# The outer exponential of a megakernel's attention in three blocks a group instead of seven units

## The chip, the cores and the metric

The kernel runs on one NeuronCore of one Trainium2 chip, as one launch. The metric is the device time in microseconds; the runs of the kernel before took 256.16, 258.83 and 258.78 us, median 258.78.

## What is computed

The input is x, 32 x 32 x 16 x 25 in float32. Three layers follow each other: a graph and temporal convolution block (L0), an attention layer and a recurrent layer with a batch norm in front of it. All weights are small, 32 x 32 for the most part. Only the attention matters for this change. Each of the 32 batches has 400 tokens (16 x 25) of 32 channels:

```
t = layernorm(t) over channels
Q = (t @ rot) @ WqT;  K = (t @ ent) @ WkT;  V = t @ WvT
dist2 = |Q|^2 + |K|^2 - 2 Q K^T
scores = exp(-dist2)                 # the inner exponential
attn   = softmax(scores, axis=keys)  # the outer exponential, then its sum
t = t + attn @ V
```

So two exponentials are taken of every one of 400 x 400 pairs of tokens in each batch. Behind it stands `t + ffn(layernorm(t))`, where the recurrence needs W x normalised with mean and variance over all tokens.

## The kernel before, in words

The 32 batches are worked in 8 groups (G) of 4 (NB). A group's channels fill the 128 partitions: 4 batches x 32 channels, 400 tokens on the free axis.

In the attention the scores lie with the keys on the partitions and the 400 queries on the free axis. A batch's 400 keys are 3 full tiles of 128 and 16 left over; the rest of all four batches shares one more tile. So a group has 13 tiles (TILES) of 128 x 400. They are handled in pairs, the units: units 0 to 5 have two tiles (800 elements a partition), unit 6 has one (400). Tiles 0 to 2 belong to batch 0, 3 to 5 to batch 1, 6 to 8 to batch 2, 9 to 11 to batch 3. The result of both exponentials, `prob`, is kept in SBUF for a whole group, twice (parity of the group).

The order is written out by hand on each engine, and semaphores count the steps:

- PE, `attend`: for each unit of group g `scores` (two bf16 matmuls per tile, in two PSUM slots that alternate; slot by slot PE waits for the inner exponential of two units before). Between these stand steps of older groups: `products(g-1, k)`, attention times V, behind units 1, 2, 4 and 5 (k = 0 to 3); `sums` and `tail_sums` of g-1 behind unit 3; `center2(g-2)` behind unit 4, `wx(g-3)` behind 5, `variance2(g-2)` behind 6. `products` with k reads the tiles k of all four batches, so k = 0 needs all up to unit 4, k = 1 and 2 up to unit 5, k = 3 unit 6. k = 0 also waits for `nrm_ready`, which is the quotient of the group before, because it overwrites the PSUM bank that the quotient reads.
- ACT, `weights`: `inner` of unit u (from PSUM to `prob`, `e1_done`), and behind it `outer` of unit u-1 (in place in `prob`, `p_ready`). The outer of unit 6 stands behind the next group's inner of unit 0. In between stand the three steps of the second layernorm, `norm2`: logarithm and exponential of group g-3 at units 0 and 1, square of g-2 at unit 4.
- DVE, `attend`: `add_tiles` of units 0 to 5 sums a batch's three full tiles (two adds a batch, `part_sum`); behind unit 0 `norm2(g-3)`; behind unit 2 `reciprocals(g-1)`, 2.65 us long, and `stats(g-3)` (bn_stats); behind unit 4 `quotient(g-1)` and `residual(g-1)`. `variance2(g-2)` on PE waits for `stats(g-3)`.

The first group's units are mixed with the last steps of the layers before (lines around L498). The instructions of the trace carry these lines: inner L457, outer L464, adds L671, reciprocal L680, quotient L687, bn_stats L701, scores L930, sums L941, tail sums L947, products L959 and L963, variance L976.

Of the kernel before, what the change touches and what calls it, by code (L numbers as in the profile page):

```python
# [32 lines left out]
G = B // NB  # L33
# [14 lines left out]
FULL = N // P  # L48
TAIL = N - FULL * P

TILES = NB * FULL + 1
UNITS = (TILES + 1) // 2
ADDS = NB * (FULL - 1)
PROB = TILES * N
RB = 8
# [24 lines left out]
def build(nc, x_tok, x, consts, out):  # L80
    with ExitStack() as ctx:
# [9 lines left out]
        def c_(name, rows=P):  # L91
            o, w = COLUMNS[name]
            return cst[0:rows, o:o + w]
# [53 lines left out]
        prob = [arena[:, o:o + PROB].rearrange("p (k n) -> p k n", k=TILES) for o in (0, at_1)]  # L147
# [72 lines left out]
        def tiles(u):  # L220

            return 2 * u, min(2 * u + 2, TILES)

        def slot(par, u):

            return (par * UNITS + u) % 2

# [15 lines left out]
        def _(sp):  # L243
# [22 lines left out]
            def load_operands(i, par):  # L266

                g = 2 * i + par
                sp.wait_ge(kq_stored[par], 96 * i + 96 + CREDIT_DMA)
                sp.wait_ge(e_stored, 16 * i + 16 + CREDIT_DMA)  # L270
                for dst, scratch, n in ((ka, dka, 4), (qa, dqa, 4), (kb, dkb, 2), (qb, dqb, 2)):
                    sp.dma_start(dst[par][0:n * C, :, :], scratch[bass.ds(g, 1)].rearrange(
                        "o (b c) (s n) -> (c s) (o b) n", b=NB, n=N)).then_inc(operands_in[par], 16)
                rows = de[bass.ds(i, 1)].rearrange("o (g h b r) n -> g h r (o b) n", g=2, h=2, b=NB)
                for h, (dst, row) in enumerate(((kb, 2 * C), (qb, 2 * C + 3))):
                    sp.dma_start(dst[par][row:row + 3, :, :], rows[par, h, 0:3]).then_inc(operands_in[par], 16)
# [17 lines left out]
            with sp.Fori(1, PAIRS) as i:  # L294
                for par in range(2):
                    sp.wait_ge(s_done, UNITS * (2 * i + par - 1))
                    load_operands(i, par)
# [65 lines left out]
        def _(act):  # L363
# [88 lines left out]
            def inner(g, par, u):  # L452

                act.wait_ge(s_done, UNITS * g + u + 1)
                lo, hi = tiles(u)
                o = 2 * slot(par, u)
                nc.scalar.activation(prob[par][:, lo:hi, :], ps[:, o:o + hi - lo, 0:N], ACT.Exp,  # L457
                                     scale=2.0).then_inc(e1_done, 1)

            def outer(g, par, u):  # L460
                act.wait_ge(e1_done, UNITS * g + u + 1)
                lo, hi = tiles(u)
                p = prob[par][:, lo:hi, :]
                nc.scalar.activation(p, p, ACT.Exp).then_inc(p_ready, 1)  # L464

            def norm2(g, step, banks=NORM_BANKS):

                if step == 0:
                    act.wait_ge(centered2, g + 1)
                    nc.scalar.activation(sq2, ps[:, banks[0], 0:N], ACT.Square).then_inc(sq2_ready, 1)  # L470
                elif step == 1:
                    act.wait_ge(var2_done, g + 1)
                    if banks[0] != NORM_BANKS[0]:
                        act.wait_ge(xl2_ready, g + CREDIT1)
                    nc.scalar.activation(rs2, ps[:, banks[1], 0:N], ACT.Ln, bias=c_("eps")).then_inc(ln2_ready, 1)
                else:
                    act.wait_ge(ln2_ready, g + 1)
                    nc.scalar.activation(rs2, rs2, ACT.Exp, scale=-0.5).then_inc(rs2_ready, 1)

            def weights(g, par):  # L480
                since = g if isinstance(g, int) else G
                if since > 1:
                    act.wait_ge(pv_done, g - 1)
                for u in range(UNITS):
                    if since == 1 and u == 2:
                        for h in range(2):
                            act.wait_ge(kq_stored[h], 96 * PAIRS + CREDIT_DMA)
                    inner(g, par, u)
                    if u:
                        outer(g, par, u - 1)  # L490
                    elif since > 0:
                        outer(g - 1, 1 - par, UNITS - 1)
                    if u in (0, 1) and since > 2:
                        norm2(g - 3, u + 1)
                    if u == 4 and since > 1:
                        norm2(g - 2, 0)


            for step, first, end in ((squares, 0, 2), (inverse_roots, 2, 3), (kq_firsts, 3, 5),
                                     (v_and_squares, 5, UNITS)):  # L500
                step(PAIRS - 1)
                for u in range(first, end):
                    inner(0, 0, u)
                    if u:
                        outer(0, 0, u - 1)
            for g in range(1, 4):
                weights(g, g % 2)
            with act.Fori(2, PAIRS) as i:
                for par in range(2):
                    weights(2 * i + par, par)  # L510
            outer(G - 1, 1, UNITS - 1)
            for step in range(1, 3):
                norm2(G - 3, step)
            for g in (G - 2, G - 1):
# [32 lines left out]
        def _(dve):  # L547
# [109 lines left out]

            def add_tiles(g, par, u):

                dve.wait_ge(p_ready, UNITS * g + u + 1)  # L660
                for t in range(*tiles(u)):
                    b, k = divmod(t, FULL)
                    if b == NB or k == 0:
                        continue
                    dst = psum[:, par, b, :]
                    if k == 1:
                        a = prob[par][:, t - 1, :]
                    else:
                        a = dst
                        dve.wait_ge(part_sum, ADDS * g + (FULL - 1) * b + k - 1)  # L670
                    nc.vector.tensor_tensor(dst, a, prob[par][:, t, :], ALU.add).then_inc(part_sum, 1)  # L671
# [31 lines left out]
            def attend(g, par):  # L703

                since = g if isinstance(g, int) else G
                if since > 1:
                    dve.wait_ge(psum_used, g - 1)
                for u in range(UNITS - 1):
                    add_tiles(g, par, u)
                    if since > 2 and u == 0:  # L710
                        norm2(g - 3)
                    if since > 0 and u == 2:
                        reciprocals(g - 1, first=since == 1)
                    if since > 2 and u == 2:
                        stats(g - 3)
                    if since > 0 and u == 4:
                        quotient(g - 1, first=since == 1)
                        residual(g - 1)
# [85 lines left out]
        def _(pe):  # L804
# [130 lines left out]
            def sums(g, par, first):  # L935

                pe.wait_ge(part_sum, ADDS * (g + 1))
                if not first:
# [4 lines left out]
                last.then_inc(psum_used, 1)  # L943

            def tail_sums(g, par):
                pe.wait_ge(p_ready, UNITS * (g + 1))
                mm_(ps[:, 5, 0:N], c_("tail_ones"), prob[par][:, TILES - 1, :], start=False, stop=True,  # L947
                    skip_group_check=True).then_inc(sums_done, 1)

            def products(g, par, k, first):  # L950

                if k == 0:
                    pe.wait_ge(vb_ready, g + 1)
                    if not first:
                        pe.wait_ge(nrm_ready, g)

                pe.wait_ge(p_ready, UNITS * g + (TILES - 1 - FULL + k) // 2 + 1)
                if k == FULL:
                    mm_(ps[:, 4, 0:N], vb[:, par, P * k:P * k + P], prob[par][:, TILES - 1, :], start=False, stop=True,  # L959
                        skip_group_check=True).then_inc(pv_done, 1)  # L960
                    return
                for b in range(NB):
                    mm_(ps[C * b:C * b + C, 4, 0:N], vb[:, par, P * k + C * b:P * k + C * b + C],  # L963
                        prob[par][:, FULL * b + k, :], start=(k == 0), stop=False, skip_group_check=True)
# [47 lines left out]
            with pe.Fori(2, PAIRS) as i:  # L1012
                for par in range(2):
                    g = 2 * i + par
                    pe.wait_ge(operands_in[par], 96 * i + 96)
                    attend(g, par)
            products(G - 1, 1, 0, False)
            center2(G - 2, LAST_BANKS[G - 2])
            wx(G - 3)
            sums(G - 1, 1, False)  # L1020
            tail_sums(G - 1, 1)
            variance2(G - 2, LAST_BANKS[G - 2])
            for k in range(1, FULL + 1):
                products(G - 1, 1, k, False)
# [139 lines left out]
```

## Time and profile before

| | |
|---|---|
| runs, us | 256.16, 258.83, 258.78 |
| median, us | 258.78 |
| span of the profiled execution, us | 256.3 |
| what lies around the span | not given apart; the lowest run is as long as the span |
| attention stage, groups 0 to 7 | about 90 to 193 us of the span |
| recurrence, from | 218.3 us |
| PE, ACT, DVE busy | 81%, 67%, 59% |
| mean granted clock of TensorE | 0.944 |

The page gives busy shares for the whole span, and forty slices of it. A stage of the kernel is read from the timeline of an engine, where each row has the start, the time until the result is written, and in brackets how long the engine stood idle before it and who ended that. Two rows of ACT or DVE overlap by some 0.1 us, so the price of an instruction in a row of them is the distance between starts, not its duration. Who waits for its result waits for the duration. The chain of waits follows the work that ended last backwards, and so names the instructions on which the end depends.

### The profile page before, as it was taken

Reading aid. Unit: us, or ns where it says so; the run is one execution under the profiler, and the core shown is the slowest. Engines: PE = TensorE matmul, PEld = TensorE weight load, DVE = VectorE, ACT = ScalarE, POOL = GpSimd, SP = SyncE. Lnnn points to the kernel's source line nnn. Section 1 sums busy time; section 2 is a strip of 40 time slices with the busy share of each in tenths; the row PEclk is TensorE's granted clock in tenths of the full one; section 3 lists DMA queues with packets and bytes.
Section 4 is the critical chain, followed back from the end, with each engine's and each line's share of the span. In section 5 each row is a group of like instructions: output and inputs, shape, how many; then the busy total and the mean of one; then the engine's idle time right before and its main releaser. Section 6 shows DMA issues by size and latency. Waiting matters only on the chain.

```text
span 256.3 us, 4008 instructions
## 1 busy us (share of the span) xinstructions
PE 208.7 (81%) x1186; PEld 106.6 (42%) x1186; DVE 151.3 (59%) x284; ACT 170.7 (67%) x307; POOL 27.5 (11%) x44
## 2 busy tenths in 40 slices
PE   0395998998998979598999899999995944998950
PEld 0272653643643535123334333334332211987850
DVE  0147639929929915959667777777776544001560
ACT  2127398599499598979899898989894222254540
POOL 6000000260140050521010100001000000000000
PEclk9997999999999999979999999999998895599996
DMA  6910010096994091786451606070000000000006
GB/s 246 299 45 27 14 54 0 8 314 197 295 306 136 30 330 42 255 267 173 97 163 35 192 2 182 18 194 1 0 0 0 0 0 0 3 0 0 0 8 251
DMA packets 26881, 26.81 MB, mean 105 GB/s; under 512 B 1550, under 2 KB 25806, under 8 KB 26740
## 3 DMA queue, kind: packets, MB, share of 16 engines
q1 hardware_dynamic: 26724, 25.51, 33.8%
q10 hardware_dynamic: 144, 1.13, 1.3%
q8 instruction: 7, 0.11, 0.2%
q14 instruction: 6, 0.05, 0.1%
HBM read 14.74 MB, written 11.88 MB: 104 GB/s over the span
## 4 chain that ended last, share of the span: by engine, by line
PE 39%; DVE 21%; ACT 19%; issue 9%; DMA 6%; SPq 3%; DVEq 0%; ACTq 0%
DVE arena L680 6%; ACT arena L457 5%; PE ps L1045 5%; PE ps L1050 5%; DVE arena L598 5%; ACT arena L464 5%; PE ps L930 4%; PE ps L856 3%; DMA cst<-consts 3%; PE ps L832 3%; SPq L261 2%; ACT arena L389 2%; PE ps L842 2%; PE ps L868 2%; PE ps L976 2%
## 5 line engine op out<-in xcount | busy, mean ns | idle before, releaser
L457 ACT ACTIVATE arena<-ps 128x800 f32<-128x800 f32 (+1 forms) x56 | 44.4, 795 | 8.1 <-PE ps L930 6.4
L464 ACT ACTIVATE arena<-arena 128x800 f32<-128x800 f32 (+1 forms) x56 | 46.3, 828 | 0.0
L930 PE MATMUL ps<-qa,ka 128*128 128x400 bf16 (+1 forms) x128 | 35.4, 340 | 3.2 <-ACT arena L457 2.9
L930 PE MATMUL ps<-qb,kb 96*128 96x400 bf16 (+1 forms) x128 | 35.3, 338 | 0.0
L671 DVE TENSOR_TENSOR psum<-arena 128x400 f32<-128x400 f32 x32 | 19.6, 611 | 14.7 <-ACT arena L464 14.7
L533 ACT ACTIVATE yb<-ps,small 128x160 f32 x40 | 13.8, 391 | 16.5 <-PE ps L1050 16.2
L671 DVE TENSOR_TENSOR psum<-psum,arena 128x400 f32<-128x400 f32 x32 | 19.5, 609 | 7.1 <-ACT arena L464 6.0
L963 PE MATMUL ps<-arena,vb 128*32 128x400 f32 x192 | 21.8, 530 | 1.2 <-issue 1.2
L680 DVE RECIPROCAL arena<-ps 128x400 f32<-128x400 f32 x8 | 21.2, 2651 | 1.3 <-PE ps L947 1.3
L930 PEld LDWEIGHTS ps<-qa,ka 128*128 128x128 bf16 (+1 forms) x128 | 10.4, 97 | 27.6 <-ACT arena L457 11.8
L856 PE MATMUL ps<-arena,cst 128*128 128x400 f32 x32 | 14.6, 584 | 6.5 <-DVE arena L598 6.5
L1045 PE MATMUL ps<-xl,wsc 128*128 x80 | 16.3, 331 | 2.2 <-DVE yb L766 1.2
L598 DVE COPY arena<-arena 32x400 f32<-32x400 f32 x48 | 17.2, 358 | 0.9
L1050 PE MATMUL ps<-yb,cst 128*128 x80 | 17.1, 340 | 0.0
L1045 PEld LDWEIGHTS ps<-xl,wsc 128*128 128x128 f32 x80 | 13.4, 211 | 3.2 <-issue 3.2
L616 DVE TENSOR_TENSOR arena<-ps,arena 128x400 f32<-128x400 f32 x8 | 4.2, 569 | 17.2 <-ACT arena L417 17.2
L930 PEld LDWEIGHTS ps<-qb,kb 96*128 96x128 bf16 (+1 forms) x128 | 10.4, 98 | 8.9 <-issue 4.9
L331 POOL TENSOR_TENSOR arena<-arena,cst 128x400 bf16<-128x400 f32 x4 | 4.6, 1146 | 86.6 <-ACT arena L436 86.6
L1050 PEld LDWEIGHTS ps<-yb,cst 128*128 128x128 f32 x80 | 13.2, 209 | 1.2
L402 ACT ACTIVATE t<-arena,small 128x400 f32 (+1 forms) x8 | 4.8, 629 | 12.7 <-DVE arena L608 12.7
L856 PEld LDWEIGHTS ps<-arena,cst 128*128 128x128 f32 x32 | 5.5, 202 | 15.2 <-DVE arena L598 14.5
L778 DVE TENSOR_TENSOR outs<-t,yb x10 | 7.4, 737 | 6.8 <-ACT yb L533 6.8
(138 smaller groups left out, 358.8 us busy)
## 6 DMA issues: line engine op xcount, KB each, us to landing
dka<-arena SPq DMA_DIRECT2D x16, 200.0 KB, 3.0
dqa<-arena SPq DMA_DIRECT2D x16, 200.0 KB, 3.1
ka<-dka SPq DMA_DIRECT2D x8, 400.0 KB
qa<-dqa SPq DMA_DIRECT2D x8, 400.0 KB
arena<-x_tok SPq DMA_DIRECT2D x4, 400.0 KB
t<-x SPq DMA_DIRECT2D x1, 1600.0 KB, 12.6
dkb<-arena SPq DMA_DIRECT2D x8, 200.0 KB, 3.3
dqb<-arena SPq DMA_DIRECT2D x8, 200.0 KB, 4.3
```

The lines of the kernel that those rows point to most:

```text
L457: nc.scalar.activation(prob[par][:, lo:hi, :], ps[:, o:o + hi - lo, 0:N], ACT.Exp, scale=2.0).then_inc(e1_done, 1)
L464: nc.scalar.activation(p, p, ACT.Exp).then_inc(p_ready, 1)
L533: nc.scalar.activation(yb[:, bass.ds(s + 1, 1), 4 * h:4 * h + 4, :].rearrange("p o g c -> p (o g c)"), ps[:, 4 * h + bank, 0:HALF], ACT.Si ...
L598: last = nc.vector.tensor_copy(*tap_input(par, j, k))
L671: nc.vector.tensor_tensor(dst, a, prob[par][:, t, :], ALU.add).then_inc(part_sum, 1)
L680: nc.vector.reciprocal(rden, ps[:, 5, 0:N]).then_inc(rden_ready, 1)
L832: last = mm_(ps[NB * CH * h:NB * CH * (h + 1), 2 * par, MT * tt:MT * tt + MT], xk[par][0:MT, o:o + NB * CH], mlo[:, h, :], start=True, sto ...
L856: mm_(ps[:, 2 * par + 1, 0:N], cst[:, o + P * j:o + P * j + P], tap_in[par][j], start=(j == 0), stop=False)
L930: last = mm_(ps[row:row + keys, bank, 0:N], kk[par][0:rows, b, o:o + keys], qq[par][0:rows, b, :], start=first, stop=not first, skip_group ...
L963: mm_(ps[C * b:C * b + C, 4, 0:N], vb[:, par, P * k + C * b:P * k + C * b + C], prob[par][:, FULL * b + k, :], start=(k == 0), stop=False, ...
L1045: mm_(ps[:, 4 * h + bank, 0:HALF], wsc[:, :], xl2[:, 4 * h:4 * h + 4, bass.ds(NC * s, NC)], start=True, stop=False)
L1050: mm_(ps[:, 4 * h + bank, 0:HALF], c_("vT"), yb[:, bass.ds(s, 1), 4 * h:4 * h + 4, :].rearrange("p o g c -> p (o g c)"), start=False, stop ...
```

## The change

The seven outer exponentials of a group are taken in three blocks: units 0 and 1 (tiles 0 to 3), 2 and 3 (4 to 7), 4 to 6 (8 to 12). Block 0 is issued behind the inner exponential of unit 2, block 1 behind that of unit 4, block 2 behind the next group's inner of unit 1. `p_ready` now counts three a group, and who waited for a unit waits for its block. Nothing else is moved.

```diff
--- before.py
+++ after.py
@@ -50,6 +50,7 @@
 
 TILES = NB * FULL + 1
 UNITS = (TILES + 1) // 2
+OUTERS = ((0, 2), (2, 4), (4, 7))
 ADDS = NB * (FULL - 1)
 PROB = TILES * N
 RB = 8
@@ -221,6 +222,10 @@
 
             return 2 * u, min(2 * u + 2, TILES)
 
+        def outer_of(u):
+
+            return next(n for n, (lo, hi) in enumerate(OUTERS) if lo <= u < hi)
+
         def slot(par, u):
 
             return (par * UNITS + u) % 2
@@ -457,10 +462,11 @@
                 nc.scalar.activation(prob[par][:, lo:hi, :], ps[:, o:o + hi - lo, 0:N], ACT.Exp,
                                      scale=2.0).then_inc(e1_done, 1)
 
-            def outer(g, par, u):
-                act.wait_ge(e1_done, UNITS * g + u + 1)
-                lo, hi = tiles(u)
-                p = prob[par][:, lo:hi, :]
+            def outer(g, par, n):
+
+                first, end = OUTERS[n]
+                act.wait_ge(e1_done, UNITS * g + end)
+                p = prob[par][:, tiles(first)[0]:tiles(end - 1)[1], :]
                 nc.scalar.activation(p, p, ACT.Exp).then_inc(p_ready, 1)
 
             def norm2(g, step, banks=NORM_BANKS):
@@ -486,10 +492,10 @@
                         for h in range(2):
                             act.wait_ge(kq_stored[h], 96 * PAIRS + CREDIT_DMA)
                     inner(g, par, u)
-                    if u:
-                        outer(g, par, u - 1)
-                    elif since > 0:
-                        outer(g - 1, 1 - par, UNITS - 1)
+                    if u == 1 and since > 0:
+                        outer(g - 1, 1 - par, 2)
+                    if u in (2, 4):
+                        outer(g, par, u // 2 - 1)
                     if u in (0, 1) and since > 2:
                         norm2(g - 3, u + 1)
                     if u == 4 and since > 1:
@@ -501,14 +507,14 @@
                 step(PAIRS - 1)
                 for u in range(first, end):
                     inner(0, 0, u)
-                    if u:
-                        outer(0, 0, u - 1)
+                    if u in (2, 4):
+                        outer(0, 0, u // 2 - 1)
             for g in range(1, 4):
                 weights(g, g % 2)
             with act.Fori(2, PAIRS) as i:
                 for par in range(2):
                     weights(2 * i + par, par)
-            outer(G - 1, 1, UNITS - 1)
+            outer(G - 1, 1, 2)
             for step in range(1, 3):
                 norm2(G - 3, step)
             for g in (G - 2, G - 1):
@@ -657,7 +663,7 @@
 
             def add_tiles(g, par, u):
 
-                dve.wait_ge(p_ready, UNITS * g + u + 1)
+                dve.wait_ge(p_ready, len(OUTERS) * g + outer_of(u) + 1)
                 for t in range(*tiles(u)):
                     b, k = divmod(t, FULL)
                     if b == NB or k == 0:
@@ -943,7 +949,7 @@
                 last.then_inc(psum_used, 1)
 
             def tail_sums(g, par):
-                pe.wait_ge(p_ready, UNITS * (g + 1))
+                pe.wait_ge(p_ready, len(OUTERS) * (g + 1))
                 mm_(ps[:, 5, 0:N], c_("tail_ones"), prob[par][:, TILES - 1, :], start=False, stop=True,
                     skip_group_check=True).then_inc(sums_done, 1)
 
@@ -954,7 +960,7 @@
                     if not first:
                         pe.wait_ge(nrm_ready, g)
 
-                pe.wait_ge(p_ready, UNITS * g + (TILES - 1 - FULL + k) // 2 + 1)
+                pe.wait_ge(p_ready, len(OUTERS) * g + outer_of((TILES - 1 - FULL + k) // 2) + 1)
                 if k == FULL:
                     mm_(ps[:, 4, 0:N], vb[:, par, P * k:P * k + P], prob[par][:, TILES - 1, :], start=False, stop=True,
                         skip_group_check=True).then_inc(pv_done, 1)
```

ACT at the border between two groups, before (line 457 is `inner`, 464 `outer`, 475 and 478 the second layernorm's logarithm and exponential):

```order
L457 ACTIVATE arena<-ps 128x400 [waits s_done]
L464 ACTIVATE arena<-arena 128x800 [waits e1_done]
L457 ACTIVATE arena<-ps 128x800 [waits s_done,pv_done]
L464 ACTIVATE arena<-arena 128x400 [waits e1_done]
L475 ACTIVATE prep<-ps,cst 128x400 [waits var2_done]
L457 ACTIVATE arena<-ps 128x800 [waits s_done]
L464 ACTIVATE arena<-arena 128x800 [waits e1_done]
L478 ACTIVATE prep<-prep 128x400 [waits ln2_ready]
L457 ACTIVATE arena<-ps 128x800 [waits s_done]
L464 ACTIVATE arena<-arena 128x800 [waits e1_done]
```

ACT at the same place now (462 is `inner`, 470 `outer`):

```order
L462 ACTIVATE arena<-ps 128x800 [waits s_done]
L462 ACTIVATE arena<-ps 128x400 [waits s_done]
L462 ACTIVATE arena<-ps 128x800 [waits s_done,pv_done]
L481 ACTIVATE prep<-ps,cst 128x400 [waits var2_done]
L462 ACTIVATE arena<-ps 128x800 [waits s_done]
L470 ACTIVATE arena<-arena 128x2000 [waits e1_done]
L484 ACTIVATE prep<-prep 128x400 [waits ln2_ready]
L462 ACTIVATE arena<-ps 128x800 [waits s_done]
L470 ACTIVATE arena<-arena 128x1600 [waits e1_done]
```

The outer of unit 5 that stood between the inner exponentials of unit 6 and 0, that of unit 6 behind unit 0 and that of unit 0 behind unit 1 are gone; the block of units 4 to 6, 2000 elements wide, stands behind the inner exponential of unit 1, and the new group's first outer comes a unit later.

PE behind the second unit of scores of a group, now (936 is `scores`, 969 `products`; the order of PE is the same as before):

```order
L936 MATMUL ps<-qa,ka 128x400 [waits e1_done]
L936 MATMUL ps<-qb,kb 128x400
L936 MATMUL ps<-qa,ka 128x400
L936 MATMUL ps<-qb,kb 128x400
L969 MATMUL ps<-arena,vb 32x400 [waits p_ready,nrm_ready,vb_ready]
L969 MATMUL ps<-arena,vb 32x400 x3
L936 MATMUL ps<-qa,ka 128x400 [waits e1_done]
L936 MATMUL ps<-qb,kb 128x400
L936 MATMUL ps<-qa,ka 128x400
```

Nothing moved here. What `p_ready` stands for did: before, it was unit 4 of the group before at this place, now it is the block of units 4 to 6.

## Rows read from the trace of the kernel before

**Rows 1.** The page: the span, and each engine's busy time.

```profile
span 256.3 us, 4008 instructions
...
PE 208.7 (81%) x1186; PEld 106.6 (42%) x1186; DVE 151.3 (59%) x284; ACT 170.7 (67%) x307; POOL 27.5 (11%) x44
```

**Rows 2.** The chain of waits in order of time: start us, us on the chain, what.

```profile
177.05 2.25 DVE arena L680
...
179.62 0.53 DVE stat L701
...
180.28 0.91 PE ps L976 x2
...
188.57 0.59 DVE psum L671
```

**Rows 3.** ACT's timeline: start us, us, engine, line, operation, out<-in, [idle before <-releaser].

```profile
112.07 0.84 ACT L457 ACTIVATE arena<-ps 128x800 f32<-128x800 f32 x1 [1.28 <-DMA dqb<-arena]
...
134.96 0.84 ACT L457 ACTIVATE arena<-ps 128x800 f32<-128x800 f32 x1
...
181.91 0.84 ACT L457 ACTIVATE arena<-ps 128x800 f32<-128x800 f32 x1 [0.91 <-PE ps L930]
182.65 0.53 ACT L464 ACTIVATE arena<-arena 128x400 f32<-128x400 f32 x1
183.07 0.59 ACT L475 ACTIVATE prep<-ps,cst 128x400 f32<-128x400 f32 x1
183.55 0.84 ACT L457 ACTIVATE arena<-ps 128x800 f32<-128x800 f32 x1
184.27 0.88 ACT L464 ACTIVATE arena<-arena 128x800 f32<-128x800 f32 x1
185.03 0.54 ACT L478 ACTIVATE prep<-prep 128x400 f32<-128x400 f32 x1
185.45 0.84 ACT L457 ACTIVATE arena<-ps 128x800 f32<-128x800 f32 x1
```

**Rows 4.** PE's timeline, around products and sums of one group.

```profile
181.03 0.33 PE L930 MATMUL ps<-qa,ka 128*128 128x400 bf16 x1
...
182.49 0.88 PE L963 MATMUL ps<-arena,vb 128*32 128x400 f32 x8
...
185.69 0.88 PE L941 MATMUL ps<-psum,cst 128*32 128x400 f32 x8
186.50 0.94 PE L947 MATMUL ps<-arena,cst 128*128 128x400 f32 x2
187.28 0.33 PE L930 MATMUL ps<-qa,ka 128*128 128x400 bf16 x1
```

**Rows 5.** DVE's timeline, reciprocal, add and quotient.

```profile
189.68 2.65 DVE L680 RECIPROCAL arena<-ps 128x400 f32<-128x400 f32 x1
...
193.26 0.57 DVE L671 TENSOR_TENSOR psum<-psum,arena 128x400 f32<-128x400 f32 x1
193.75 0.56 DVE L687 TENSOR_TENSOR sq<-ps,arena 128x400 f32<-128x400 f32 x1
```

**Rows 6.** Groups of ACT by form: line engine op, shapes xcount | busy us, mean ns | idle before.

```profile
L464 ACT ACTIVATE arena<-arena 128x800 f32<-128x800 f32 x48 | 42.1, 877 | 0.0
...
L464 ACT ACTIVATE arena<-arena 128x400 f32<-128x400 f32 x8 | 4.3, 532 | 0.0
```

**Rows 7.** PE's timeline behind three idle stretches.

```profile
94.57 0.94 PE L880 MATMUL ps<-arena,prep 128*128 128x400 f32 x2 [1.70 <-DVE arena L616]
...
106.39 0.33 PE L930 MATMUL ps<-qa,ka 128*128 128x400 bf16 x1 [2.69 <-ACT arena L457]
...
197.04 1.67 PE L970 MATMUL ps<-t,cst 128*128 128x400 f32 x2 [1.74 <-DVE xl L695]
```

**Rows 8.** Windows of PE: stretch, us, PE busy (count), PEclk, DMA share, GB/s.

```profile
108.30:111.70 3.40, 3.40 (x17) 0.51 0.97 331
...
197.10:200.50 3.40, 3.40 (x8) 0.51 0.00 0
```

## The prediction

> **What bounds the kernel now.** I read the page first. ACT is busy 67% of the span and PE 81% [rows 1], so neither share alone says what holds the attention stage, and the stage has to be read as a ring. The chain of waits in order of time gives it [rows 2]: reciprocal of a group, then bn_stats, then the variance matmul, then the first scores of the next group, then the exponentials, then two adds, then the next reciprocal. ACT's timeline gives the period: the inner exponential of unit 2 starts at 134.96 in group 3 and at 185.45 in group 7, four groups in 50.49 us, 12.62 each [rows 3]. The same rows add up to it: 177.05 to 185.45 from reciprocal to unit 2's inner exponential (8.40), 3.12 on to the adds at 188.57, 1.11 on to the next reciprocal at 189.68 [rows 2, 3, 5]. That is 12.63. In this ring the outer exponentials of units 6, 0 and 1 lie on ACT one after another, and only unit 2's has somebody waiting for it at once. PE is never held by an outer exponential: it meets products(g, 0) behind the scores of unit 1 of the next group, long after the unit 4 that it reads has been done.
>
> **The change, part by part.**
>
> *Fewer instructions.* Outers of 800 elements start 0.76 us before the next instruction on ACT (184.27 to 185.03), one of 400 elements 0.42 (182.65 to 183.07) [rows 3]. So 400 elements cost 0.34 and an instruction by itself 0.08. Four fewer in each of 8 groups are 32 x 0.08 = 2.6 us of ACT. A merged one lasts, by 532 and 877 ns [rows 6] and so 345 ns for each 400 more, about 1.57 us (1600) and 1.91 us (2000). These are extrapolations in one direction; at 300 or 390 ns instead of 345 the ring below changes by under 0.4 us. ACT still has idle time in every group, and others wait for what it writes. Here the page "Perfetto Trace Analysis" of the Trainium skill, section "Optimizing Scalar/DVE Operations", has two rules. Grouping helps if the engine is saturated (it puts 93 ns on a ScalarE instruction in SBUF, an estimate of 3.0 us for 32); if the engine isn't saturated and makes bubbles on others, breaking instructions up may finish work sooner. By the first the sum would be about minus 3, by the second a loss; my rows speak for the second.
>
> *The results come later.* This is the term that decides. The last block of a group (units 4 to 6) is computed behind the inner exponential of unit 1 of the next group. Before, units 4 and 5 were ready long before that. Three things want them:
> - PE's products(g, 0), in order behind scores(g+1, 1) and ahead of scores(g+1, 2), which ACT needs next. Behind PE's wait stand the scores, the sums and all else.
> - DVE's adds of unit 4, and behind them on DVE the quotient of group g-1. products(g, 0) waits for that quotient too.
> - The reciprocal, which stands behind the adds of unit 2; these now wait for the block of units 2 and 3, which runs behind inner exponential 4, not 3.
>
> So the old ring takes the new waits in. From one reciprocal to the next, at the full clock:
> 1. Reciprocal to inner exponential 1: 177.05 to 183.55 is 6.50 [rows 2, 3], less the outer of unit 6 that went from there, 0.42: 6.08. It holds variance and first scores, 180.28 to 181.91.
> 2. That inner 0.72 (183.55 to 184.27), the block of 2000 elements 1.91, and 0.04 until its reader starts (the 3.12 above less 0.72, 0.76, 0.72 and 0.88): 2.67.
> 3. Add 0.49 (193.26 to 193.75), quotient 0.57 [rows 5], and 0.13 to PE (bn_stats ends at 180.15, PE starts at 180.28 [rows 2]): 1.19.
> 4. PE from products 0 to the scores of unit 4: 182.49 to 187.28, 4.79, which holds two products, scores 2 and 3, sums and tail sums [rows 4]. Then the scores of unit 4, 0.88 (1.63 from variance to inner exponential less the 0.75 of the variance's own step, 180.28 to 181.03): 5.67. ACT can't be faster here, since inner exponentials 3 and 4 need those scores.
> 5. Inner exponential 4, 0.72, block of 1600 elements 1.57, and 0.04: 2.33.
> 6. Two adds, 188.57 to 189.68: 1.11.
>
> Sum 19.05, against 12.62: **6.4 us more a group**. Groups 3 to 7 are reached by four such rings: 25.7.
>
> *Before the ring is whole.* From unit 2 of group 1 to that of group 3 took 22.89 (112.07 to 134.96) [rows 3]. Group 1 to 2 anew: 3.98 to inner 4 (step 4 less 0.81 and 0.88), 0.72 and 1.42 for it and the block's place on ACT, 0.84 and 0.9 for inner 5 and the next scores, 0.74, then 2.67, 1.19, 0.81 and 0.88: 14.2. Group 2 to 3 adds a square, a logarithm and part of the variance, 15.6. Together 6.9 more. Reaching unit 2 of group 1: the block has to be waited for, about 3 us, but ACT has 1.28 idle for a DMA there, and arrives about a microsecond earlier: 1.8 more, at most 3, at least 0. At the end, from unit 2 of group 7 to its reciprocal, steps 4 to 6 give 7.4 in place of 4.2: 3.2 more; the path behind is as before.
>
> Sum at the full clock: 1.8 + 6.9 + 25.7 + 3.2 = **37.6**.
>
> *The clock.* PE now stands idle twice in a ring: about 2.5 us between the scores of unit 6 and the variance, which waits for bn_stats (scores 4 to 6 with what stands between them are some 5.0 us of PE's steps; by steps 4 to 6 and rows 2 the variance starts 0.88 + 2.33 + 1.11 + 3.23 = 7.55 after scores 4 do), and about 4.4 us ahead of products 0 (the last block 1.95, inner 1 and logarithm 1.2, add and quotient 1.2). In the trace before, an idle stretch of 2.69 us was followed, within two microseconds of its end, by 3.4 us at 0.51 of the clock, that is at 1.2 and not 2.4 GHz, one of 1.74 by the same again, one of 1.70 by nothing [rows 7, 8]. So I expect a low stretch in every ring. It costs half its length where PE is on the ring: 1.7 us in step 4. For variance and first scores (1.63) I count half of a second one, 0.8. That is 1.7 for each of the two early groups and 2.5 for each of four rings: **13.4**. From below the price is 0; from above it is all of PE's work on the ring at half clock, 4.79 + 0.88 + 1.63 = 7.3 a ring more, but no low stretch on busy PE here was so long; two whole ones of 3.4 plus the first scores give 4.9 a ring, 23 in all. The page "TensorE: Matmul & The Clock Gate" of the Trainium skill, Part 1, says that the low clock is the default and activity lifts it, which would make the low stretches come in every ring; the rows above agree, but show it only at single places.
>
> *What is hidden.* Nothing moves on SP and POOL. Operand loads wait for the scores of the group before, now later but with a longer group to land in. The blocks write the same tiles in place.
>
> Total 37.6 + 13.4 = 51.0. The profiled execution has a span of 256.3, about the lowest run (256.16); the median of the three runs is 2.5 above it. Against the span the new time is 307.3; with a part of that distance I say **308**.
>
> **The rivals.**
> A. *The forecast*, ring and low stretches: 299 to 318. **0.74**.
> B. *The ring at the full clock*: 256.3 + 37.6, so 293 to 299. For it: idle of 1.70 left the clock alone. Against it: 4.4 us is longer than any idle stretch that stayed free. **0.08**.
> C. *A shorter ring*: bn_stats is not the last thing the variance waits for, and the leg over the reciprocal drops out. Then a group takes inner 4 to inner 5 to the next scores, as in group 2 to 3, 15.6 to 16.4, and 4 x 2.7 to 4 x 3.4 go away: 280 to 284, with low stretches to 292. Against it: that leg already ends the wait before the variance, and its inputs come later now. **0.08**.
> D. *Worse*: both low stretches whole in every ring, or a wait that I have not seen: above 318. **0.07**.
> E. *Not slower*: ACT sets the pace, and the 32 saved starts come off: 256.3 - 2.6 = 253.7, at the least gain the same time. This is the grouping rule above. It decides at PE's products 0: it needs the last block to be done when PE gets there. But the block starts behind inner exponential 1, which reads the scores that PE has just finished, so it ends 0.72 + 1.91 us later at the least; PE would have to take matmuls out of order. **0.03**.
>
> "Faster", "same" and "slower" are meant at 1%, about what a measurement of this kernel can tell from no change. Faster and same share E: 0.02 and 0.01; slower 0.97. The range takes A and B and leaves C, D and E out: 293 to 318, 0.82.
>
> **What the new profile would show.** ACT's outer instructions: 24, mean 1.57 and 1.91 us. Step 1 to 6: 19 us at least from one unit 2 to the next in groups 3 to 7, near 21.5 with the low clock. PE's wait for the quotient (DVE) ahead of products 0, 4 us and more in each group, and one for bn_stats ahead of the variance of about 2.5. In the chain, products, sums and quotient would appear, which are not in it now. PEclk would show 0.5 to 0.9 all through the stage. I am wrong if groups come every 12 to 13 us, if PE's idle time ahead of products is under a microsecond, or if the clock stays at 1.0.

## The result, and the profile after

The change takes 1.206 times as long as the kernel before, 95% interval 1.197 to 1.216: median 313.85 us of four runs (308.83 to 314.36), against 258.07 before. Ratios here and below are taken over undisturbed runs alone (of the change only two, 313.41 and 308.83 us, which makes it 53 us slower), so they can differ from the quotient of two medians. The profiled execution has a span of 311.6 us, 55.3 more than the 256.3 before. The forecast was 308, with a range of 293 to 318.

The page first: span, busy times, and the slices of the granted clock.

```profile
span 311.6 us, 3962 instructions
...
PE 229.4 (74%) x1186; PEld 109.7 (35%) x1186; DVE 150.2 (48%) x284; ACT 169.4 (54%) x275; POOL 28.4 (9%) x44
...
PEclk9997999999999959596876875975967969559996
```

Before, ACT was busy 67% [rows 1]; now it is 54%, and its busy time is 1.3 us shorter (169.4 against 170.7). What was added on ACT is waiting. PE, with the same 1186 matmuls, is busy 229.4 us in place of 208.7, and PEclk now lies between 0.5 and 0.9 in most slices of the attention stage.

ACT by form: the merged instructions (line 470 is `outer` now). Last columns are the count, busy time, mean ns, and the idle time before them.

```profile
L462 ACT ACTIVATE arena<-ps 128x800 f32<-128x800 f32 x48 | 39.8, 838 | 59.6 <-PE ps L936 59.4
L470 ACT ACTIVATE arena<-arena 128x1600 f32<-128x1600 f32 x16 | 24.5, 1531 | 0.0
L470 ACT ACTIVATE arena<-arena 128x2000 f32<-128x2000 f32 x8 | 15.0, 1872 | 0.0
```

They took 1.53 and 1.87 us, where [rows 6] extrapolated to 1.57 and 1.91. Ahead of the inner exponentials of 800 elements ACT stands idle for 59.4 us in all, waiting for scores; before it was 5.1.

ACT's timeline, inner exponential of unit 2 in groups 1, 2, 3 and 7. It answers to the first two lines and the last of [rows 3].

```profile
113.76 0.84 ACT L462 ACTIVATE arena<-ps 128x800 f32<-128x800 f32 x1 [3.27 <-PE ps L936]
...
130.15 0.84 ACT L462 ACTIVATE arena<-ps 128x800 f32<-128x800 f32 x1 [4.23 <-PE ps L936]
...
148.45 0.84 ACT L462 ACTIVATE arena<-ps 128x800 f32<-128x800 f32 x1 [3.82 <-PE ps L936]
...
237.18 0.84 ACT L462 ACTIVATE arena<-ps 128x800 f32<-128x800 f32 x1 [4.04 <-PE ps L936]
```

Group 1 starts 1.69 us later than before. Groups 1 to 3 take 34.69 us in place of 22.89, the four groups from 3 to 7 take 88.73 in place of 50.49, so 22.18 each, and all behind unit 2 of group 7 takes 74.4 in place of 70.9. That is 1.7 + 11.8 + 38.2 + 3.6 = 55.3, the whole difference.

The chain of waits through one ring, from reciprocal to reciprocal. Columns: start us, us on the chain, what (L686 reciprocal, L707 bn_stats, L982 variance, L470 outer, L693 quotient, L969 products, L462 inner, L677 add).

```profile
200.77 0.37 DVE arena L686
...
203.34 0.53 DVE stat L707
...
204.00 1.43 PE ps L982 x2
...
208.74 1.89 ACT arena L470
...
211.23 0.58 DVE sq L693
...
211.93 1.56 PE ps L969 x8
...
220.30 0.84 ACT arena L462
...
222.59 0.59 DVE psum L677
...
223.70 0.37 DVE arena L686
```

Quotient, products and the block of 2000 elements are in it, as the prediction's steps 2 to 4 had them; in the ring of [rows 2] none of these was on the chain. PE's two stalls in the timeline show the same.

```profile
204.00 1.43 PE L982 MATMUL ps<-sq,cst 128*128 128x400 f32 x2 [2.49 <-DVE stat L707]
...
211.93 1.56 PE L969 MATMUL ps<-arena,vb 128*32 128x400 f32 x8 [3.98 <-DVE sq L693]
```

PE stood 3.98 us ahead of products 0, for the quotient, and 2.49 us ahead of the variance, for bn_stats; the prediction had 4.4 and 2.5. Products 0 took 1.56 us, against the 0.88 of [rows 4]. The windows of PE over this and the next ring tell why. Columns as in [rows 8].

```profile
204.00:207.90 3.90, 3.90 (x10) 0.56 0.95 262
207.90:211.90 4.00, 0.05 (x1) 0.90 0.00 0
211.90:214.00 2.10, 2.07 (x10) 0.50 0.00 0
214.00:217.80 3.80, 3.80 (x15) 0.50 0.00 0
217.80:226.90 9.10, 6.64 (x41) 0.99 0.00 0
226.90:230.00 3.10, 3.07 (x10) 0.70 0.00 0
230.00:234.00 4.00, 0.09 (x1) 0.50 0.00 0
234.00:238.50 4.50, 4.36 (x20) 0.51 0.00 0
```

The clock has two levels, 0.5 of full speed (1.2 GHz) and full speed (2.4 GHz); a value between is a window with a change of level in it. Windows of a quarter of a microsecond (not shown) place the changes. This ring has two low stretches, 204.2 to 207.7 and 211.1 to 217.9: 3.4 us behind the stall ahead of the variance, 6.8 around the end of the stall ahead of products. The next ring has one, 228.1 to 238.4: 10.2 us, with a whole stall in it. The two rings before these do the same (3.4 and 6.8 us, then 10.2). So rings of 22.9 and of 21.5 us follow each other; the reciprocals start at 156.43, 179.31, 200.77, 223.70 and 245.16. The 3.4 us of [rows 8] is the length of one of the low stretches only.

### The profile page after: what moved, and what is told of

The parts are those of the page before. It is cut to its first block, busy times and chain, and to the rows that moved or that the text cites. A ratio compares the mean times of both kernels' runs of the same rounds, so it can differ in the third digit from the quotient of the medians.

```text
span 311.6 us, 3962 instructions
## 1 busy us (share of the span) xinstructions
PE 229.4 (74%) x1186; PEld 109.7 (35%) x1186; DVE 150.2 (48%) x284; ACT 169.4 (54%) x275; POOL 28.4 (9%) x44
## 4 chain that ended last, share of the span: by engine, by line
PE 48%; ACT 18%; DVE 16%; issue 10%; DMA 4%; SPq 2%; DVEq 0%; ACTq 0%
PE ps L936 10%; ACT arena L470 7%; PE ps L969 7%; PE ps L1051 4%; DVE arena L604 4%; PE ps L1056 4%; ACT arena L462 4%; PE ps L862 2%; DMA cst<-consts 2%; PE ps L838 2%; PE ps L953 2%; DVE arena L686 2%; PE ps L982 2%; PE ps L947 2%; SPq L266 2%
## 5 line engine op out<-in xcount | busy, mean ns | idle before, releaser
L462 ACT ACTIVATE arena<-ps 128x800 f32<-128x800 f32 (+1 forms) x56 | 43.6, 791 | 63.8 <-PE ps L936 63.6
L969 PE MATMUL ps<-arena,vb 128*32 128x400 f32 x192 | 31.0, 734 | 27.2 <-DVE sq L693 24.3
L936 PE MATMUL ps<-qa,ka 128*128 128x400 bf16 (+1 forms) x128 | 41.6, 388 | 3.0 <-ACT arena L462 3.0
L677 DVE TENSOR_TENSOR psum<-arena 128x400 f32<-128x400 f32 x32 | 19.4, 606 | 48.9 <-ACT arena L470 48.9
L936 PE MATMUL ps<-qb,kb 96*128 96x400 bf16 (+1 forms) x128 | 41.5, 386 | 0.0
L470 ACT ACTIVATE arena<-arena 128x1600 f32<-128x1600 f32 (+1 forms) x24 | 39.5, 1645 | 0.0
L677 DVE TENSOR_TENSOR psum<-psum,arena 128x400 f32<-128x400 f32 x32 | 19.2, 599 | 29.5 <-ACT arena L470 28.6
L936 PEld LDWEIGHTS ps<-qa,ka 128*128 128x128 bf16 (+1 forms) x128 | 11.6, 106 | 37.0 <-issue 19.1
L686 DVE RECIPROCAL arena<-ps 128x400 f32<-128x400 f32 x8 | 21.2, 2650 | 1.1 <-PE ps L953 1.1
L862 PE MATMUL ps<-arena,cst 128*128 128x400 f32 x32 | 14.6, 584 | 6.5 <-DVE arena L604 6.5
L969 PEld LDWEIGHTS ps<-arena,vb 128*32 128x32 f32 x192 | 4.7, 128 | 39.9 <-issue 39.9
L982 PE MATMUL ps<-sq,cst 128*128 128x400 f32 x16 | 8.9, 644 | 13.0 <-DVE stat L707 12.4
L936 PEld LDWEIGHTS ps<-qb,kb 96*128 96x128 bf16 (+1 forms) x128 | 11.7, 108 | 12.0 <-issue 9.2
L346 POOL COPY vb<-vst 128x384 f32 (+1 forms) x8 | 5.1, 640 | 107.7 <-PE ps L965 107.7
```

What stands on the lines that cost most here:

```text
L686: nc.vector.reciprocal(rden, ps[:, 5, 0:N]).then_inc(rden_ready, 1)
L862: mm_(ps[:, 2 * par + 1, 0:N], cst[:, o + P * j:o + P * j + P], tap_in[par][j], start=(j == 0), stop=False)
L936: last = mm_(ps[row:row + keys, bank, 0:N], kk[par][0:rows, b, o:o + keys], qq[par][0:rows, b, :], start=first, stop=not first, skip_group ...
L982: mm_(ps[:, banks[1], 0:N], c_("mean"), sq2, start=True, stop=True).then_inc(var2_done, 1)
```

## Experiments

Each kernel was timed beside the kernel before (medians 257.3 to 258.0). The ring time is read from the reciprocals or quotients in the chain of waits.

**The last three units single again.** Units 0-1 and 2-3 stay merged. The table says behind which inner exponential (key) which block is issued, and whether it is the group's before (1).

```diff
-OUTERS = ((0, 2), (2, 4), (4, 7))
+OUTERS = ((0, 2), (2, 4), (4, 5), (5, 6), (6, 7))
+BEHIND = {0: ((4, 1),), 2: ((0, 0),), 4: ((1, 0),), 5: ((2, 0),), 6: ((3, 0),)}
...
-                    if u == 1 and since > 0:
-                        outer(g - 1, 1 - par, 2)
-                    if u in (2, 4):
-                        outer(g, par, u // 2 - 1)
+                    for n, lag in BEHIND.get(u, ()):
+                        if lag == 0:
+                            outer(g, par, n)
+                        elif since > 0:
+                            outer(g - 1, 1 - par, n)
```

> Units 0-1 and 2-3 stay merged, units 4, 5 and 6 are single again at the places they had before. Ring theory: products no longer wait for a late block nor for the quotient behind it; what stays is the reciprocal behind a later add (the block of units 2 and 3 runs behind inner exponential 4). From reciprocal to inner 1 6.5 us, to inner 2 1.14, to inner 4 2.86, block and adds 2.33 + 1.11: 13.9 a group, 14.0 to 14.6 with PE's own work, against 22.2 with the change and 12.6 before; total 270 to 280 us, the upper part if the low clock still comes in each group. Rival, that only the last block does harm: 12.6 a group and 256 to 259 us. Rival, that merging as such starves ACT of scores: 18 us a group or more, above 290.

Measured: 277.48 us, ratio 1.076 (1.067 to 1.084). So merging units 0 to 3 by itself costs 20 us, and the last block brings the other 34 of the 53. The rival that only the last block does harm is out. The rings are 14.5 to 16.1 us in this kernel's trace, so partly above the 14.0 to 14.6 expected; the kernel with the early block, below, has the same two lengths, and there the difference is shown to be the clock's.

**Only the last block merged.** Units 0 to 3 single, at their old places.

```diff
-OUTERS = ((0, 2), (2, 4), (4, 7))
+OUTERS = ((0, 1), (1, 2), (2, 3), (3, 4), (4, 7))
+BEHIND = {1: ((4, 1), (0, 0)), 2: ((1, 0),), 3: ((2, 0),), 4: ((3, 0),)}
```

> Only units 4 to 6 are merged, behind the next group's inner exponential 1; units 0 to 3 are single at their old places. Ring theory: the late block, add, quotient and PE's run from products 0 stay in the ring, but the reciprocal goes back to its old distance from unit 2. 16.8 us a group at the full clock, 19 with low stretches; total 286 to 300. Rival, that the last block does all the harm: as the change, 22 a group and 313. Rival, that it is the middle block (reciprocal): near 13 a group and 262.

Measured: 302.49 us, ratio 1.175 (1.166 to 1.184), a little above the expected 300. Quotients in the chain of waits of this kernel:

```profile
146.20 0.58 DVE sq L696
...
164.89 0.58 DVE sq L696
...
184.56 0.58 DVE sq L696
...
222.51 0.58 DVE sq L696
```

19.1 us a group on average. Alone the last block costs 45 us, alone the two others 20, together 53: they share the ring, and their costs do not add.

**Quotient ahead of the block's add.** The change, with two lines of DVE at another unit.

```diff
-                    if since > 0 and u == 4:
+                    if since > 0 and u == 2:
                         quotient(g - 1, first=since == 1)
                         residual(g - 1)
```

> The change, with quotient and residual of group g-1 on DVE ahead of the adds of units 3 and 4 instead of behind that of unit 4. Ring theory: add 0.49 and quotient 0.57 leave the path from the late block to products 0, which then wait for the block alone: 1.1 us less a group over six groups, total 305 to 308. Rival, that PE's wait is for the block anyway and the quotient hides in it: the same 313. Rival, that the quotient, which needs products 3 of the group before, now holds up DVE's adds and so the sums: 316 or more.

Measured: 307.43 us, ratio 1.195 (1.186 to 1.203). That is 6.4 us less by the medians, but the interval overlaps that of the change (1.197 to 1.216), so the times alone do not tell the two apart; the traces do. PE's waits ahead of products in the stage, in total, how often and the longest, for the change and for this kernel:

```profile
PE ps L969 <- DVE sq L693: 24.3, 6, 4.4
```

```profile
PE ps L969 <- ACT arena L470: 19.8, 7, 3.4
```

They name the block now (ACT L470), not the quotient, and the stall ahead of products is 2.7 us in the rings of 20.2 to 20.7 us where it was 4.0. So the quotient behind the add was on the path. Step 3 gave it 1.1 us; but these rings (by the reciprocals, which are not shown) are 1.7 us shorter on average than the 22.2 of the change. What the rest of the 1.7 is was not taken apart; the low stretches lie at other places of the ring in this kernel.

**The same block, earlier.** Three blocks as in the change, the last one behind inner exponential 6 of its own group.

```diff
-                    if u == 1 and since > 0:
-                        outer(g - 1, 1 - par, 2)
-                    if u in (2, 4):
+                    if u in (2, 4, 6):
                         outer(g, par, u // 2 - 1)
```

> Three blocks as in the change, but the last one behind inner exponential 6 of its own group, so three instructions a group at once, and no lateness for products and quotient. Ring theory: what decides is when a block is ready and not how many there are: the late block, add, quotient and PE's run leave the ring; what stays is the reciprocal behind a later add and ACT's three inner exponentials in a row, for whose scores PE needs 1.5 us each. 14.6 a group at the full clock, total 270 to 280, as with the last three single. Rival, that the number of merged units decides: near the change, 305 or more. Rival, that three instructions at last pay: 257 or less.

Measured: 277.91 us, ratio 1.076 (1.071 to 1.082), the same as with the last three units single. Three instructions a group or five make no difference that these runs show; 34 us come from where the block stands. Reciprocals in the chain of waits:

```profile
134.11 2.65 DVE arena L683
...
148.99 2.65 DVE arena L683
...
165.04 0.38 DVE arena L683
...
181.15 0.37 DVE arena L683
...
195.66 0.37 DVE arena L683
```

The distances are 14.9, 16.1, 16.1 and 14.5. The ring at the full clock, 14.6, is there in two of four; the other two take 1.5 us more. The only stall left in these rings is that of 2.49 us ahead of the variance.

**PE kept busy.** The change, with matmuls into a PSUM bank that is free at that moment, overwritten before anyone reads it. No result depends on them; the work is only added.

```diff
+DUMMY = (5, 3)
...
+            def busy(bank, count):
+                for _ in range(count):
+                    mm_(ps[:, bank, 0:N], c_("center"), cst[:, 0:N], start=True, stop=True,
+                        skip_group_check=True)
...
+                    if since > 1 and u == 1:
+                        pe.wait_ge(rden_ready, g - 1)
+                        busy(5, DUMMY[0])
                     if since > 0 and u in PRODUCTS_AT:
...
                     if since > 1 and u == 6:
+                        pe.wait_ge(e1_done, UNITS * g + 6)
+                        busy(2 * slot(par, 5), DUMMY[1])
                         variance2(g - 2)
```

> The change as it is, with PE given matmuls that nobody reads in its two idle stretches, 5 of 128x400 float32 ahead of products 0 (3.4 us) and 3 ahead of the variance (2.0 us). Clock theory: the granted clock stays at 1.0 in the attention stage, a group takes 19.1 us as worked out for the full clock in place of 22.2, total 293 to 299. Rival, that the clock falls for another reason, or that it isn't what separates 19.1 from 22.2: clock 0.85 again and 310 to 320, or more since the added work stands in front of the rest.

Measured: 299.71 us, ratio 1.168 (1.157 to 1.178), clear of the change's 1.206 (1.197 to 1.216): 10 us less by the ratios, 14.1 by the medians, 15.3 by the spans of the two profiled executions. And this with 2.28 + 3.52 us more of matmuls in a ring by its timeline, which leave stalls of 0.28 and 1.22 us. The window over the stage, and the reciprocals:

```profile
112.00:235.00 123.00, 114.02 (x595) 47.25 (x588) 59.16 (x83) 73.18 (x84) 6.92 (x12) 0.98 0.24 63
```

```profile
175.19 0.38 DVE arena L687
...
194.35 0.37 DVE arena L687
...
213.51 0.37 DVE arena L687
...
232.67 0.37 DVE arena L687
```

Its clock column is 0.98; over the same window of the change it is 0.78. The three distances are 19.16 each; steps 1 to 6 of the prediction gave 19.05. The median is a hair above the expected 299. Steps 1 and 4, those with PE's work in them, take 6.07 us (194.35 to 200.42) and 5.67 (204.45 to 210.12) here; the prediction had 6.08 and 5.67 for the full clock. The price of the low clock is thus 22.2 less 19.2, 3.0 us a ring.

**One stall filled at a time.** `DUMMY = (5, 0)`, ahead of products alone.

> The change, with PE's idle time filled only ahead of products 0 (5 matmuls). The change loses 3.1 us a group to the low clock (22.2 against 19.16 with both stalls filled). Theory that the long stall ahead of products brings most of it: 19.5 to 20.5 us a group, 300 to 305 us in all. Rival, that each stall by itself is enough to let the clock fall for the same length: 21 to 22 a group, 308 to 313. Rival, that one stall filled keeps the clock up through the other, 296 to 300.

Measured: 304.33 us, ratio 1.184 (1.177 to 1.191). And `DUMMY = (0, 3)`, ahead of the variance alone:

> The change, with PE's idle time filled only ahead of the variance (3 matmuls), the 4 us ahead of products left idle. Theory that the long stall brings most of the loss, in products and scores behind it: 21.3 to 22 us a group, 308 to 312, since only variance and first scores (0.8 us on average) are mended. Rival, that the short stall begins the low stretches: below 303.

Measured: 309.66 us, ratio 1.203 (1.196 to 1.209). The reciprocals of the two, in this order:

```profile
174.90 0.38 DVE arena L687
...
194.66 0.37 DVE arena L687
...
213.83 0.37 DVE arena L687
...
234.40 0.37 DVE arena L687
```

```profile
182.24 0.38 DVE arena L687
...
202.97 0.38 DVE arena L687
...
223.63 0.38 DVE arena L687
...
244.20 0.37 DVE arena L687
```

The first is clear of the change; the second is not told apart from it by its time, since the intervals overlap. By the rings, filling the long stall gives 2.4 us (19.8 on average) and filling the short one 1.5 (20.7), together more than the 3.0 of both. The savings overlap: with the short stall filled, the low stretches behind the long one last 3.4 us in the last three groups (from 192.5, 213.0 and 233.5), where in the change they lasted 6.8 and 10.2. Filling one stall also shortens the low stretch at the other. The 20.7 lie below the 21.3 to 22 that I expected. The total came out as expected all the same, because this kernel is later in its early groups: its third reciprocal starts at 161.26, the change's at 156.43. Why is open.

**Early block, stall filled.** The kernel with the block behind inner exponential 6, and three such matmuls ahead of the variance.

> The kernel with the last block behind inner 6 of its own group (277.9 us, groups of 14.5 to 16.1), with PE's one stall, ahead of the variance, filled by 3 matmuls. Clock theory: groups of 14.5 to 15.0 throughout and 272 to 275 us. Rival, that the alternation of 14.5 and 16.1 has another cause: 277 to 280.

Measured: 273.95 us, ratio 1.064 (1.058 to 1.070), where the kernel without the fill has 1.076 (1.071 to 1.082). Reciprocals:

```profile
165.19 0.38 DVE arena L684
...
179.69 0.37 DVE arena L684
...
194.20 0.37 DVE arena L684
```

14.5 throughout, and again to the next at 208.70. The clock has no low stretch between 130 and 229 us here. So the 1.5 us in some rings were the clock's.

**Out of the old ring instead.** The kernel before, without any merge, and the variance behind the next group's first scores.

```diff
                     scores(g, par, u)
+                    if since > 2 and u == 0:
+                        variance2(g - 3)
...
-                    if since > 1 and u == 6:
-                        variance2(g - 2)
...
+            variance2(G - 3)
             products(G - 1, 1, 0, False)
```

> The kernel before, with the variance matmul of the second layernorm behind the first scores of the next group instead of ahead of them; no exponential is merged. Ring theory: the old ring (12.62) loses the variance's 0.75 us between bn_stats and those scores, which no longer wait for it; the next ring or PE's own work takes over near 12.0 us a group. Four to five groups at 0.6: 2.5 to 3 us faster, 254 to 255. Rival, that PE's or ACT's own work already sets 12.6: no change. Rival, that the logarithm now waits on ACT, in order, for the later variance: 1 to 3 us slower.

Measured: ratio 0.980 (0.974 to 0.987), median 255.55. Faster, clear of no change, but by how much is less clear: the six runs lie between 251.47 and 256.65 us, and their median is 0.9% below the 257.96 of the kernel before. The ring shows it better. From the third reciprocal to the seventh this kernel takes 47.4 us, the kernel before 50.5, so 11.9 in place of 12.62 a group and 3.1 us in all; 12.0 and 2.5 to 3 were worked out. With quotient and residual moved as above besides:

> As the one with the late variance, and also quotient and residual ahead of the adds of units 3 and 4. Ring theory: they are not in the ring here, so at most 1 us from the first groups, 253.5 to 255. Rival: the quotient waits for products 3 and holds up three adds and the sums behind them, slower than the late variance alone by 1 to 4 us.

Measured: ratio 0.980 (0.975 to 0.986), median 253.77. Not told apart from the one without. These two beat both kernels.

**One merge where nobody waits long.** To the last kernel, the block of units 5 and 6 behind the next group's inner exponential 0.

```diff
+OUTERS = ((0, 1), (1, 2), (2, 3), (3, 4), (4, 5), (5, 7))
+BEHIND = {0: ((5, 1),), 1: ((0, 0),), 2: ((1, 0),), 3: ((2, 0),), 4: ((3, 0),), 5: ((4, 0),)}
```

> The same with one merge where nobody waits long: units 5 and 6 in one block of three tiles behind the next group's inner exponential 0, seven starts of outer instructions become six. Ring theory: neither gain nor loss against the same kernel without the merge, within 0.5 us, since ACT's 0.08 us a group is no longer in the ring and products 1 want unit 5 only a step later. Theory that fewer instructions pay as such: 0.6 us faster. Rival, that every merge costs: 1 us slower or more.

Measured: ratio 0.986 (0.981 to 0.992), median 254.82. Its interval overlaps that of the kernel without the merge, so neither a gain nor a loss of half a per cent is shown, and a loss of 1 us, the rival's, isn't excluded. Its logarithms on ACT (line 482) show the same ring as without the merge:

```profile
156.71 0.59 ACT L482 ACTIVATE prep<-ps,cst 128x400 f32<-128x400 f32 x1
...
168.59 0.59 ACT L482 ACTIVATE prep<-ps,cst 128x400 f32<-128x400 f32 x1
...
180.53 0.59 ACT L482 ACTIVATE prep<-ps,cst 128x400 f32<-128x400 f32 x1
```

11.9 us apart.

## Why the prediction was right, and what was off

The sign, the ring and its members were right. By its own steps, the ring from 200.77 to 223.70 measures (the last column is what the prediction gave):

| step | measured, us | predicted, us |
|---|---|---|
| 1 reciprocal to inner exponential 1 | 7.25 | 6.08 |
| 2 inner 1 and block of 2000 | 2.72 | 2.67 |
| 3 add, quotient, to products | 1.19 | 1.19 |
| 4 PE from products 0 to inner 4 | 8.37 | 5.67 |
| 5 inner 4 and block of 1600 | 2.29 | 2.33 |
| 6 two adds | 1.11 | 1.11 |
| ring | 22.93 | 19.05, with the clock 21.55 |

(Inner exponential 1 starts at 208.02 and the block's add at 210.74 in the timelines of ACT and DVE, which are not shown.) The steps on ACT and DVE came out to 0.05 us. Steps 1 and 4 hold PE's work, and are longer by 1.2 and 2.7; in the kernel with both stalls filled they take 6.07 and 5.67, so this is the clock.

The term that was mis-sized is the clock's share in step 4. In the rings of 22.9 us step 1 is 1.2 longer than at the full clock and step 4 2.7; in those of 21.5 it is 0.3 and 2.0 (179.31 to 185.72, 189.73 to 197.37). The 0.8 for variance and first scores was half of a low stretch by guess; it came out on average, 0.75, because it is nearly whole in every second ring and small in the others. Step 4 got 1.7, half of a low stretch of 3.4 us, and the average is 2.3, since the low stretches cover 6.0 and 4.3 us of the work behind the stall. I had also put 1.7 on each of the two early groups, where 16.39 + 18.30 against 14.2 + 15.6 leaves 2.4 each. Of the 4.3 us between 51.0 and 55.3 the clock makes 1.5 in the early groups and 2.5 in the four rings (38.2 against 25.7 + 10.0), if the ring at the full clock is taken as predicted; 0.4 came at the end, and the start was 0.1 too long.

Two readings in the prediction were off. It set the span of 256.3 beside the lowest run. In all later runs the time is 1.7 to 2.2 us above the span (313.41 and 311.6 for the profiled execution of the change), so the 0.7 us added for this was about a microsecond short, and that is the rest of the distance between 308 and 313.41. And against rival B it said that 4.4 us is longer than any idle stretch that stayed free. The trace before has one at its start: PE stands 9.71 us ahead of its first matmul, and the granted clock is 1.0 until 22.9 us. The length of an idle stretch alone doesn't tell whether the clock falls.

What the merge saves can't be seen any more: the 2.6 us were distances between starts on an engine that has work, and ACT now waits. The outer instructions last 39.5 us together and lasted 46.3 before (24.5 + 15.0, and 42.1 + 4.3 in [rows 6]), but ACT's busy time, which counts overlapping instructions once, fell by 1.3 us only. No kernel with a merge beat its like without.

Rival B, the full clock, was wrong for the change; its ring came once PE had work in both stalls. Rival C fell with the chain, which goes over reciprocal and bn_stats in each of the four rings. Rival E fell at the place where it was to be decided, ahead of products 0. The Trainium skill's rule for an engine that isn't saturated ("Perfetto Trace Analysis", "Optimizing Scalar/DVE Operations": breaking instructions up may let work be done sooner if the engine makes bubbles on others) agrees with these runs, though they show it from the other side: merging made the bubbles, and nothing was cut finer than before. Its rule on grouping names saturation as the condition; ACT was busy 67% of the span here, and no run shows a kernel in which ACT was saturated.

What stays open: why the low stretch at one stall gets shorter when the other stall is filled. Which of the two late blocks of units 0 to 3 costs the 20 us was not tried; by the chain it is that of units 2 and 3.

## What to carry to other kernels

Merging instructions on an engine saves a start each (here 0.08 us), but every reader of a piece now waits for the last piece. Before merging, write down for each piece who reads it and how long it had lain ready, and walk the ring from a late reader back to the producer: if it closes, the delay is paid once in every turn. Where an in-order engine stalls for it, look for a second price in its clock; and where a ring sets the time, look for a member that can step out of it, which gave 1 to 2% here for one moved matmul.

## What the runs showed of the hardware

Matmuls that nobody reads made the kernel faster, 1.168 in place of 1.206 times the kernel before: the granted clock from 112 to 235 us rose from 0.78 to 0.98. Stalls of 2.5 us could let it fall, but did not each time. In the kernel with the early block PE stands 2.49 us ahead of each variance. Around or within 2 us of the end of the stalls that end at 152.22, 168.27, 198.89 and 215.01 the clock fell to 1.2 GHz; behind the one that ends at 184.38, of the same length, it did not, and the ring took 14.5 us in place of 16.1. With the stall filled no ring behind 150 us was long (14.5 each), and the ratio went from 1.076 to 1.064. And an activation's time beyond 800 elements grew a little slower than from 400 to 800: 1.53 us for 1600 and 1.87 for 2000 against 1.57 and 1.91 by the line through the two shorter ones (0.53 and 0.88 us).
